# Graph network kernel on one core: the stages of its first pass over the edges set further apart

## The reference

```python
def _L0_gnn_ref(x, edge_index, mlp_w1, mlp_b1, mlp_w2, mlp_b2, conv_w, conv_b):
    row, col = (edge_index[0], edge_index[1])
    edge_feat = jnp.concatenate([x[row], x[col]], axis=-1)
    h = jax.nn.gelu(edge_feat @ mlp_w1 + mlp_b1, approximate=False)
    edge_weight = jax.nn.sigmoid(h @ mlp_w2 + mlp_b2)[:, 0]
    ...
    deg = jax.ops.segment_sum(ew_f, col_f, num_segments=n)
    dinv = jnp.where(deg > 0, jax.lax.rsqrt(deg), 0.0)
    norm = dinv[row_f] * ew_f * dinv[col_f]
    ...
    out = jax.ops.segment_sum(msg, col_f, num_segments=n)
    return out + conv_b
...
h = jnp.maximum(_layernorm(x, axis=-1), 0.0)
x = x + _L0_gnn_ref(h, edge_index, ...)
...
```

## Time and profile before

| | us |
|---|---|
| median of 3 runs | 5144.15 (5142.53 to 5153.06) |
| the profiled execution | 5117.41 |
| its span in the trace | 5115.6 |
| TensorE busy | 3731.3 (73%) |
| VectorE busy | 2360.6 (46%) |
| GpSimd busy | 2177.9 (43%) |
| ScalarE busy | 807.9 (16%) |

### The profile page before, as it was taken

How to read it: one execution, slowest core, us unless ns; L and a number is a source line. 1 busy time by engine, 2 the same in 40 slices (tenths; PEclk the granted TensorE clock), 3 DMA queues, 4 the chain that set the end, 5 groups by cost and what they waited for, 6 DMA issues and landing times.

```text
span 5115.6 us, 81513 instructions
## 1 busy us (share of the span) xinstructions
PE 3731.3 (73%) x26476; PEld 2547.5 (50%) x26476; DVE 2360.6 (46%) x11373; ACT 807.9 (16%) x2506; POOL 2177.9 (43%) x1749
## 2 busy tenths in 40 slices
PE   4444444444456666108999698899999999999999
PEld 3333333333345555105656365566666666666666
DVE  6555555555579998302223325734443333332111
ACT  1122111111125555100000001211110000000000
POOL 3556666666678888888888860000000000000000
PEclk7555555555559999559999899999999999999999
DMA  4777777777769996227777573355555665665665
GB/s 122 250 235 230 232 230 225 241 234 234 232 173 233 233 232 136 0 0 184 177 179 180 126 198 110 113 161 165 168 166 177 189 190 181 190 190 181 199 197 167
DMA packets 557026, 928.52 MB, mean 182 GB/s; under 512 B 175004, under 2 KB 412012, under 8 KB 549836
## 3 DMA queue, kind: packets, MB, share of 16 engines
q1 hardware_dynamic: 389580, 833.79, 50.9%
q0 software_dynamic: 162496, 87.75, 12.0%
q10 hardware_dynamic: 4544, 1.77, 0.2%
HBM read 741.60 MB, written 181.47 MB: 180 GB/s over the span
## 4 chain that ended last, share of the span: by engine, by line
PE 43%; POOL 20%; another core or an unknown queue 17%; issue 9%; DVE 4%; DMA 3%; ACT 3%; SPq 0%; ACTq 0%; POOLq 0%; DVEq 0%
PE ps L1006 35%; POOL adj L662 19%; DMA adj<-count,place 3%; PE ps L1040 1%; PE ps L916 1%; PE ps L907 1%; ACT gelu L719 1%; ACT tanh_half L724 1%; PE ps L1016 1%; PE ps L992 1%; PE ps L1052 1%; PE ps L1029 1%; PE ps L1049 1%; DVE summed_f L1470 1%
## 5 line engine op out<-in xcount | busy, mean ns | idle before, releaser
L1006 PE MATMUL ps<-parts,halves 128*128 128x384 bf16 x14602 | 2488.1, 326 | 296.4 <-DMA halves<-adj 296.4
L1006 PEld LDWEIGHTS ps<-parts,halves 128*128 128x128 f16 x14602 | 1431.9, 98 | 1182.1 <-DMA halves<-adj 242.7
L662 POOL DMA_INDIRECT adj<-count,place x832 | 1315.8, 1581 | 264.0 <-issue 236.3
L654 POOL DMA_INDIRECT rows<-table,src_of x880 | 837.0, 951 | 575.8 <-DVE pre L1306 279.9
L1470 DVE TENSOR_REDUCE summed_f<-ps 128x128 f32<-128x384 f32 x335 | 186.9, 558 | 1688.6 <-PE ps L1016 1145.8
L916 PE MATMUL ps<-dst_mlp,onehot_t 128*128 x2640 | 364.5, 232 | 470.4 <-ACT onehot_t L714 284.5
L916 PEld LDWEIGHTS ps<-dst_mlp,onehot_t 128*128 128x128 bf16 x2640 | 274.5, 104 | 550.4 <-issue 491.6
L801 ACT COPY source_t<-ps 128x128 f32<-128x128 f32 x196 | 52.0, 265 | 2072.1 <-PE ps L1029 2061.2
L930 PE MATMUL ps<-weight_parts,onehot_b 128*128 128x4 bf16 x880 | 132.4, 184 | 284.8 <-DVE weight_parts L1333 150.0
L747 ACT ACTIVATE onehot<-plain,norm 128x128 f32<-128x128 bf16 x880 | 281.0, 390 | 227.5 <-DVE norm L1376 120.6
L714 ACT COPY onehot_t<-ps 128x512 bf16<-128x512 bf16 x220 | 128.7, 585 | 1137.0 <-remote 967.8
(11 more groups left out here) (250 smaller groups left out, 3485.8 us busy)
## 6 DMA issues: line engine op xcount, KB each, us to landing
halves<-adj SPq DMA_DIRECT2D x289, 800.0 KB
halves<-adj SPq DMA_DIRECT2D x253, 768.0 KB
adj<-slot_of SPq DMA_DIRECT2D x53, 1568.0 KB
h_rows<-rows SPq DMA_DIRECT2D x220, 256.0 KB
rows<-h_rows SPq DMA_DIRECT2D x220, 256.0 KB
spare_sum<-key_list SPq DMA_DIRECT2D x104, 512.0 KB
onehot_list<-onehot_b SPq DMA_DIRECT2D x220, 128.0 KB
low_row<-low_list SPq DMA_DIRECT2D x220, 128.0 KB
```

The source lines that it names most:

```text
L654: nc.gpsimd.indirect_dma_start(out=rows_0[:, g % RING, s, :], out_offset=None, in_=table[:, :], in_offset=bass.IndirectOffsetOnAxis(ap=src ...
L662: nc.gpsimd.indirect_dma_start(out=adj[:, :], out_offset=bass.IndirectOffsetOnAxis(ap=place[:, k:k + 1], axis=0), in_=count16[:, k:k + 1], ...
L1006: last = nc.tensor.matmul(ps_sum[u % 3], halves[:, n % AR, c - at, :], parts[q % 2][:, c, :, :].rearrange("p t d -> p (t d)"), start=(c == ...
```

## The change

All lags of pass zero's later stages grow; no instruction is added or removed, and the buffers stay as they are. The products go from one step behind the turning to two, the addition and gelu from two to three, logits and tanh from three to four, the weights from four to six, the sum from four to seven. The argument of `compare_for` moves along with the lag of the weights, so that the key compares stay in the step in which they were.

```diff
+WEIGHED = 6
...
-            pipeline(GROUPS, [(1, copy_onehot), (3, tanh_group), (2, gelu_group), (0, clear_sums)])
+            pipeline(GROUPS, [(1, copy_onehot), (4, tanh_group), (3, gelu_group), (0, clear_sums)])
...
-            pipeline(GROUPS, [(4, sum_degrees), (1, dst_half), (0, turn_onehots)])
+            pipeline(GROUPS, [(7, sum_degrees), (2, dst_half), (0, turn_onehots)])
...
-                compare_for(g + 4, 1)
+                compare_for(g + WEIGHED, 1)
...
-            pipeline(GROUPS, [(4, write_weights), (3, reduce_logits), (2, add_halves), (0, write_onehots)])
+            pipeline(GROUPS, [(WEIGHED, write_weights), (4, reduce_logits), (3, add_halves), (0, write_onehots)])
```

## The result

The changed kernel took 5182.42 us (median of 4 runs, 5178.34 to 5190.49) beside 5143.34 us of the kernel before (4 runs, 5142.15 to 5153.06): a ratio of 1.0074, 95% interval 1.0056 to 1.0092, some 38 us. The profiled execution took 5190.49 us. The chip of this first comparison has no number on record; I call it the first.

What follows compares the result with a forecast made beforehand. GpSimd's gathers in pass zero, stalled by late additions, were taken to bound the kernel. Profiled 5117.4 us plus 1.8 us for the start gave 5119.2; with runs 26.7 us above, 5146 us, range 5020 to 5260.

Steps and rivals of the forecast that it cites:

- The forecast itself: Pass zero: gathers stay in bursts of two groups, 12.29 us each, nothing gained; 5146 us, chance 0.36.
- A microsecond of the gathers is one of the kernel: Pass zero: scatters begin 0.30 us behind the last gather, so time in GpSimd's gathers counts fully; 3655 us behind stay.
- The sum of the parts: Whole kernel: profiled 5117.4 us plus 1.8 us for the start is 5119.2; runs lie 26.7 us above, giving 5146.
- the start: Start of pass zero: first addition one step later, behind one more set of one-hot matrices and compares; 1.8 us at most.
- Two additions are done per burst, as before: Burst ends in pass zero: if products of a + 2 wait for the burst's end, two groups still take 12.29 us.
- between the two: Products of a + 2, ending some 3.4 us into a burst, lie between a prompter turning (2.2) and waiting products (6.8).
- VectorE has done its weights and logits before the products are seen, and both waits cost nothing: VectorE in bursts of two: the sum comes early, ahead of the products, so waiting for it costs 0.
- The slower rival: VectorE held by a late sum, 1.88 to 3.48 us bare per three-group burst; 43 to 156 us more, chance 0.31.
- The faster rival: Products come within the burst: bursts of three, 92 us less (5054), or all stall gone, 255 us less; chance 0.33.
- Prompt results: Pass zero: were results prompt, turning, copy, products fit within four gathers (5.0 us); kernel before some 255 us lower.
- The ports: SBUF: disjoint engine and DMA ports mean gathers shouldn't touch TensorE's work, speaking for the full gain; trace says otherwise.

Runs made afterwards that it cites:

- far_sum_only: Kernel before with only the weights moved from lag 4 to 5 and the sum from 4 to 6: 5135.31 us, ratio 1.0037 to before, second chip.
- parts4: Changed kernel with four buffers in place of two for the parts of the weights: 5131.46 us, ratio 1.0030 to the kernel before, second chip.
- after_add_first: Changed kernel with the addition put first among VectorE's stages of a step: 5104.27 us, ratio 0.9972 to the kernel before, third chip.
- near_weights: Kernel before with products, addition, gelu, logits and tanh moved as in the change, weights and sum both at 5: 5124.93 us, ratio 1.0017, second chip.

## Why the prediction was off, step by step

The measured 5182 us lie inside the range of 5020 to 5260, but that says little for the mechanism: the range took in the rivals on both sides. The forecast itself, 5146 us with bursts of two (0.36), missed by 36 us, and its pattern did not come; what came is a mixture of both rivals, in which the slower one (0.31) outweighs. That the comparison fell on a chip with late results was luck as well: on the fourth chip the changed kernel takes 4863.79 us, below the range, and has no bursts.

- **A microsecond of the gathers is one of the kernel**: right. Behind the first scatter lie 3652.5 to 3655.6 us in all fourteen profiles.
- **The sum of the parts**: the start was put at 1.8 us. The rows below show it.

The first one-hot matrices of pass zero in the timeline of before, then the same row of the changed kernel with the gather that ends its first ring wait:

```profile
124.55 0.94 DVE L1298 TENSOR_SCALAR onehot_b<-window_iota_b,local_dst 128x128 bf16<-128x128 bf16 x4
```

```profile
130.48 0.74 DVE L1300 TENSOR_SCALAR onehot_b<-window_iota_b,local_dst 128x128 bf16<-128x128 bf16 x4
...
142.69 0.94 POOL L656 DMA_INDIRECT rows<-table,src_of  x1 [16.14 <-DVE pre L1308]
```

From there to the gather are 134.95 - 124.55 = 10.40 us before and 142.69 - 130.48 = 12.21 us after, 1.81 more: right. That the wait was 16.14 us comes from a preparation that was over 5.9 us later in that execution.

- **"Two additions are done per burst, as before"**: this step failed, and with it the 5146 us. The products of a + 2 were to have to wait for the end of the burst. In 17 bursts a third addition came within it, and in 36 only one; the kernel before was locked to two in all 106. That the products lie "between the two" was read rightly, but between the two means both, and I took the one.
- **"VectorE has done its weights and logits before the products are seen, and both waits cost nothing"**: failed as well, by itself. far_sum_only shows it with near products: 42 stalls of 4.12 us at the cast, 0.37%. Nor was it quite so before, where VectorE stands at the logit reduction in 26 of the 107 stalls and at the last part of the weights in 14. I had placed the sum by the rows where it runs (906.95, promptly) and not by when VectorE hears of it.
- **The slower rival**, 0.31: right in place (VectorE at L1326 by the sum, "remote") and near in price for the single stall, wrong in how often. The 2.29 + 1.88 = 4.17 us agree with the measured mean of 4.17 by luck: 2.29 leaves out the 0.30 us that lie between any two gathers, and the 4.17 measured holds them. The bare stretch by itself was 1.95 us, against the 1.88 read. As to how often, it was 43 of 117 stalls and not each, since bursts of three were to be the rule. Hence 38 us and not 43 to 156.
- **The faster rival**, 0.33: also there in part, 40 stalls at the addition with 1.83 us in place of 2.55. Bursts of three as the rule came in no kernel; parts4 has the most, 33 of 102. after_add_first gains its 11 us in bursts of two.
- **Prompt results**: the prediction had put the kernel "some 255 us lower" with them. On the fourth chip results are prompt, the turning that ends at 901.20 being seen at 901.24, the loop turning, copy, products is short of four gathers, and the kernel before stands 281 us lower than on the first chip and 253 to 254 us lower than on the second and third. The Trainium skill, Perfetto Trace Analysis, section Tensor Engine Instruction, has the semaphore pushed once PSUM acknowledges that all bytes are written. The fourth chip agrees; the trace of before, with 174 copies released by "remote", does not.
- **The ports**: halving the traffic (quiet) or the rows of a gather (half_gather) left the lateness as it was. The Trainium skill, SBUF — State Buffer, section SBUF: two separate sides, says that engine ports and DMA ports are disjoint, and these two runs agree with it; that gathers touch nothing of TensorE's does not follow on three of the chips.

What stays open: what delays the semaphores while gathers run in pass zero, when it does not in the preparation, beside the scatters, or on the fourth chip; what the changed kernel's own ratio is on the second and third chip, as it ran on the first and the fourth alone, so that what parts4 gives back, and the gain of after_add_first over the change, are seen by the kinds of stalls (104 of 106 at the addition) and by both ratios to before, not side by side; and whether the products that come singly cost anything by themselves.

## What to carry to other kernels

Where a result comes at a moment that an engine doesn't control, what counts is what that engine has to do between the result and the step that releases the bottleneck: put this step first in its order, and then give its other stages the distance that this order needs. Here more distance between stages, with two buffers each, mostly turned a wait for one producer into a wait for another, ahead of the same step. Before costing a lag, list for each engine in order which of its waits stand ahead of the releasing instruction, and place each by when the waiting engine hears of it.

## What the runs showed of the hardware

- While gathers run back to back on GpSimd in pass zero, semaphores from TensorE, and some of VectorE's own, come late on three chips: in the kernel before some 1.9 us behind the end of each burst, though the products in the earlier trace rows were over 2.9 us ahead of it (911.59 to 914.50). The ends of TensorE's rows are modelled, but VectorE waits just so for its own instructions (102.2 us in 36 waits at L1329 in parts4). It depends neither on half of the traffic (113 or 233 GB/s) nor on the rows of a gather (64 or 128), and TensorE's loads of registers are no cause of it. What falls early in a burst is spared: in the changed kernel 109 turnings end between 1 and 2 us into their burst, and their median delay to the copy is 0.04 us. So are 24 gathers back to back in the preparation.
- On a fourth chip the same program has none of it: 0.04 us from a turning to its copy, 5.05 us a group, 4862 us. Two chips of one kind can differ by 5% in a kernel, and a change that is worth 0.74% on one is worth nothing on another.
- In the same stretches matmuls of the products, whose address comes from a register, came singly, some 0.7 us apart (665.37, 666.11, 666.84), but only where the products stand two steps back: gaps of over 0.3 us within the products number 419 in the changed kernel, 321 in parts4, 330 in after_add_first and 117 in near_weights, and none in any kernel with the products one step back, nor on the fourth chip.
